# Attention score products cut into column strips of 32 keys, with the diagonal triangles zeroed on GpSimd

## The reference, cut to what matters

```python
b, s, d = x.shape                      # 1, 4096, 256
q = (x @ Wq + bq).reshape(b, s, H, HD).transpose(0, 2, 1, 3)   # H, HD = 16, 16
k = (x @ Wk + bk).reshape(b, s, H, HD).transpose(0, 2, 1, 3)
v = (x @ Wv + bv).reshape(b, s, H, HD).transpose(0, 2, 1, 3)
mask = cols <= rows + WINDOW           # WINDOW = 128
scores = jnp.einsum('bhqd,bhkd->bhqk', q, k) / jnp.sqrt(jnp.float32(HD))
scores = jnp.where(mask[None, None], scores, -jnp.inf)
attn = jax.nn.softmax(scores, axis=-1)
out = jnp.einsum('bhqk,bhkd->bhqd', attn, v)
```

## Time and profile before

| | |
|---|---|
| time, median of 3 runs | 2160.57 us (2159.54 to 2161.64) |
| the profiled execution | 2161.43 us |
| its span, first to last instruction | 2159.7 us |
| first to last exponential of the attention | 222.7 to 1376.6 us |
| PE busy over the span | 1945.6 us (90%) |
| ACT busy over the span | 1349.6 us (62%) |
| DVE, POOL busy over the span | 457.2 us, 206.6 us |

### The profile page before, as it was taken

How to read it: one execution, slowest core, us unless ns; L and a number is a source line. 1 busy time by engine, 2 the same in 40 slices (tenths; PEclk the granted TensorE clock), 3 DMA queues, 4 the chain that set the end, 5 groups by cost and what they waited for, 6 DMA issues and landing times. The chain is left out here.

```text
span 2159.7 us, 33152 instructions
## 1 busy us (share of the span) xinstructions
PE 1945.6 (90%) x11417; PEld 870.4 (40%) x11418; DVE 457.2 (21%) x1360; ACT 1349.6 (62%) x1633; POOL 206.6 (10%) x175
## 2 busy tenths in 40 slices
PE   4863999999999999999999999766299999999995
PEld 3532322223222223222232222255266677667764
DVE  4655000000000000000000000145333333333332
ACT  2432789998989988999988999532133333333331
POOL 1000000000000000000000000146312211221121
PEclk9985999999999999999999999876599999999998
DMA  4336310000300004000000000385422212221223
GB/s 137 124 129 121 70 38 8 9 9 16 76 16 9 8 9 84 9 8 9 8 23 16 8 9 1 116 293 192 146 41 34 34 32 33 33 34 32 34 32 95
DMA packets 83767, 115.15 MB, mean 53 GB/s; under 512 B 9372, under 2 KB 75612, under 8 KB 83036
## 3 DMA queue, kind: packets, MB, share of 16 engines
q1 hardware_dynamic: 66616, 90.97, 14.9%
q0 software_dynamic: 13296, 17.80, 4.8%
q10 hardware_dynamic: 3760, 5.03, 0.8%
HBM read 73.03 MB, written 40.74 MB: 53 GB/s over the span
## 5 line engine op out<-in xcount | busy, mean ns | idle before, releaser
L1034 ACT ACTIVATE at_probs<-at_scores 128x1536 f32<-128x1536 f32 (+2 forms) x756 | 1044.8, 1433 | 113.9 <-PE at_scores L955 55.8
L952 PE MATMUL at_scores<-at_q_rows,kept_k_rows 99*128 99x512 bf16 (+3 forms) x2480 | 613.6, 362 | 10.7 <-DMA at_q_rows<-q_parts 9.4
L969 PE MATMUL at_out<-at_probs,kept_v 128*17 128x512 f32 (+3 forms) x4832 | 593.1, 567 | 0.3 <-ACT at_probs L1034 0.3
L952 PEld LDWEIGHTS at_scores<-at_q_rows,kept_k_rows 99*128 99x128 bf16 x2480 | 193.6, 98 | 621.6 <-ACT at_probs L1034 429.6
L1741 ACT ACTIVATE ex_hT<-ex_ps_hT,kept_b 128x128 f32<-128x128 f32 x568 | 154.5, 383 | 375.1 <-PE ex_ps_hT L1698 375.1
L1706 PE MATMUL ex_ps_y<-kept_w,ex_hT 128*128 x1136 | 258.7, 381 | 2.5 <-ACT ex_hT L1741 2.5
L1687 PE MATMUL ex_ps_h<-kept_w,ex_xT 128*128 x568 | 259.9, 601 | 0.9 <-DVE ex_xT L1756 0.9
L1047 DVE COPY at_out_T<-at_out 128x512 f32<-128x512 f32 x32 | 22.1, 692 | 1047.7 <-PE at_out L969 1047.7
L1706 PEld LDWEIGHTS ex_ps_y<-kept_w,ex_hT 128*128 128x128 f32 x1136 | 211.4, 191 | 28.9 <-issue 2.7
L969 PEld LDWEIGHTS at_out<-at_probs,kept_v 128*17 128x17 f32 x4832 | 82.5, 95 | 218.1 <-issue 207.8
L1666 POOL DMA_INDIRECT sums<-ex_y,ex_answer_to x71 | 110.8, 1560 | 485.8 <-DVE ex_y L1798 485.8
(11 more groups left out here) (209 smaller groups left out, 990.4 us busy)
## 6 DMA issues: line engine op xcount, KB each, us to landing
kept_w<-in_W SPq DMA_DIRECT2D x16, 1024.0 KB, 10.2
ex_x_tile<-queue SPq DMA_DIRECT2D x72, 129.5 KB, 2.0
k_parts<-kparts SPq DMA_DIRECT2D x8, 768.0 KB, 3.7
q_parts<-qparts SPq DMA_DIRECT2D x8, 768.0 KB, 3.7
at_q_rows<-q_parts SPq DMA_DIRECT2D x32, 192.0 KB
kept_k_rows<-k_parts SPq DMA_DIRECT2D x4, 1120.0 KB
x_rows<-in_x SPq DMA_DIRECT2D x4, 1024.0 KB, 14.1
kept_k_rows<-k_parts SPq DMA_DIRECT2D x8, 512.0 KB
```

The costliest lines, as they stand in the source:

```text
L952: ins = nc.tensor.matmul(out, k_rows[:, k_at + h * S + kb * P:k_at + h * S + (kb + 1) * P], q_rows[:, q:q + part], start=True, stop=not ma ...
L969: ins = nc.tensor.matmul(ps_o[h * CT:h * CT + HD + 1, first:C], v[:, kb, g * GH + h, :], probs[:, slot, column:column + width], start=i == ...
L1034: nc.scalar.activation(probs[:, c % RING, 0:width], ps_s[:, c % 2, 0:width], ACT.Exp).then_inc(exped, 1)
```

## The change

The score matmul of a block of 128 keys becomes four matmuls of 32 keys, each with its own weight load; the four write to partitions 0, 32, 64 and 96 of the same columns. The masking matmuls go, and `mask_kq` with them. In their place POOL sets the probabilities above the diagonal to zero in `probs`, in place, after the exponential: one `affine_select` for each step's pieces in a chunk (`edge_runs`), up to four heads of 128 columns. A value product of a diagonal block waits for it (semaphore `masked`). `LAG` goes from 2 to 3, so the products run one chunk later behind the scores, and the transposes too. The rest of the diff are counts of a semaphore in the setup, where one memset and one select go.

```diff
...
-            nc.gpsimd.memset(keep["mask_kq"][:], 0.0).then_inc(pool_step, 1)
             nc.gpsimd.memset(keep["mask_qk"][:], 0.0).then_inc(pool_step, 1)
-            pool.wait_ge(pool_step, 6)
-
-            nc.gpsimd.affine_select(out=keep["mask_kq"][:], in_=keep["mask_kq"][:], compare_op=ALU.is_ge, fill=MASKED,
-                                    base=0, pattern=[[1, P]], channel_multiplier=-1).then_inc(pool_step, 1)
+            pool.wait_ge(pool_step, 5)
+
...
-        LAG = 2
+        LAG = 3
...
+        def edge_runs(tile, n):
+
+            runs = []
+            for i, step in enumerate(tiles[tile]):
+                at = [column for k, h, column in pieces(tile, n) if k == i]
+                if step[0] > tile * CB and at:
+                    runs.append((at[0], step[4], len(at)))
+            return runs
+
+        masks_of = [[len(edge_runs(tile, n)) for n in range(chunks_of[tile])] for tile in range(NC)]
+
+        def masks_upto(g, tile, n):
+
+            return (g * sum(sum(m) for m in masks_of) + sum(sum(m) for m in masks_of[:tile])
+                    + sum(masks_of[tile][:n + 1]))
+
...
                     kb, first, _, _, width = tiles[tile][i]
-                    edge = kb > tile * CB
                     done = 0
                     while done < width:
                         at = column + done
                         part = min(width - done, C - at % C)
-                        out = ps_s[:, c % 2, at:at + part]
-                        masked = edge and done == 0
                         q = q_at + h * C + first + done
-                        ins = nc.tensor.matmul(out, k_rows[:, k_at + h * S + kb * P:k_at + h * S + (kb + 1) * P],
-                                               q_rows[:, q:q + part], start=True, stop=not masked)
-                        if masked:
-                            ins = nc.tensor.matmul(out[:, 0:P], ident_bf[:], mask[:], start=False, stop=True)
+                        k = k_at + h * S + kb * P
+                        for b in range(0, P, CT):
+                            ins = nc.tensor.matmul(ps_s[b:b + CT, c % 2, at:at + part], k_rows[:, k + b:k + b + CT],
+                                                   q_rows[:, q:q + part], start=True, stop=True)
                         done += part
                 ins.then_inc(scored, 1)
...
                 kb, first, width = step[0], step[1], step[4]
+                if kb > tile * CB:
+                    pe.wait_ge(masked, masks_upto(g, tile, place(step, GH - 1)[0]))
...
-                products(c - 1)
-            for upto in (len(order) - 1, len(order)):
+                products(c - LAG + 1)
+            for upto in range(len(order) - LAG + 1, len(order) + 1):
                 pe.wait_ge(exped, upto + 1)
                 products(upto)
             transposes(turn)
+
+        @block.gpsimd
+        def _(pool):
+            for c, (g, tile, n) in enumerate(order):
+                for k, (column, spacing, count) in enumerate(edge_runs(tile, n)):
+                    if k == 0:
+                        pool.wait_ge(exped, c + 2)
+                    part = probs[:, c % RING, column:column + (count - 1) * spacing + P]
+                    if count > 1:
+                        part = probs[:, c % RING, column:column + count * spacing].rearrange(
+                            "p (h q) -> p h q", h=count)[:, :, 0:P]
+                        pattern = [[0, count], [1, P]]
+                    else:
+                        pattern = [[1, P]]
+                    nc.gpsimd.affine_select(out=part, in_=part, compare_op=ALU.is_ge, fill=0.0, base=0,
+                                            pattern=pattern, channel_multiplier=-1).then_inc(masked, 1)
...
```

More of the change, by code:

```diff
@@ L221, in _ @@
                                           w[:, k].rearrange("p (h d) -> p d h", h=H)).then_inc(pool_step, 1)
-            pool.wait_ge(pool_step, 8 + 2 * KD)
+            pool.wait_ge(pool_step, 6 + 2 * KD)
         @block.scalar
@@ L298, in _ @@
             pe.wait_ge(act_step, 3)
-            pe.wait_ge(pool_step, 8 + 2 * KD)
+            pe.wait_ge(pool_step, 6 + 2 * KD)
             pe.wait_ge(w_in, 16 * 6)
@@ L827, in sem @@
             return ctx.enter_context(nc.semaphore(name))
-        ident, ident_bf, mask, v, mixed = (keep[n] for n in ("ident", "ident_bf", "mask_kq", "v", "mixed"))
+        ident, v, mixed = (keep[n] for n in ("ident", "v", "mixed"))
         CT = 32
@@ L858, in attention @@
         pv_done = sem("at_pv_done")
+        masked = sem("at_masked")
         out_read = sem("at_out_read")
@@ L1841, in adaln_attention_experts @@
             kept(inner, "ident_bf", [P, P], BF16)
-            kept(inner, "mask_kq", [P, P], BF16)
             kept(inner, "mask_qk", [P, P], BF16)
```

## The result

The changed kernel takes 2086.59 us, the median of four runs (2084.18 to 2087.97); the kernel before took 2161.11 us beside it (four runs, 2159.54 to 2162.82). The ratio is 0.9654, with a 95% interval of 0.9637 to 0.9671: faster by 74.5 us. The profiled execution is the one of 2084.18 us.

The account below looks back on a forecast made before the run. PE was taken to bound the attention stage, ACT close behind. With joins and masks gone ACT becomes the bound; its wait falls from 108 to 43 us, -65 from the median 2160.57: 2095 us, range 2076 to 2115 (66%).

Parts of the forecast that it names:

- the forecast case: Whole program: the main expectation, 2076 to 2115 us, given 66%.
- The joins: Between scores and value products on PE: 0.10 us lost at each of 2 x 574 goes, 115 us of PE time.
- The strips: Score matmuls on PE: 2480 become passes of four, 5 ns extra each, +12 us; upper end 240 ns a pass, +60 us.
- Rival A: Score strips on PE overlap only in part; halfway, 40 ns extra a pass, PE stays the bound, about 2126 us; 14%.
- Rivals B and C: PE's instruction stream limits: at 90 ns a pair, 2278 us (B, 12%); at 81 ns, unchanged at 2160 us (C, 5%).
- ACT becomes the bound: Attention stage: PE's time falls to 1024 us, under ACT's 1045, so ACT sets the pace.
- the cycle is 5.3 us against 5.57: Inner cycle of four chunks: PE needs 5.3 us, ACT's four exponentials 5.57, so PE waits some 0.27 us.
- What ACT still waits for: Attention stage: ACT's wait for PE falls from 108 us to 43 us, -65 us.
- Tile starts: Turns with the transposes and a tile's first products: ACT waits 0.7 us at each of 31 tiles, 22 us.
- Group starts: First tile of groups 1 to 3: later query loads make PE wait near 4.2 us each, 13 us for three.
- The selects and the lag: Selects on POOL: 0.6 us for 512 columns, hidden with products three chunks behind; upper end up to 20 us.
- The masks: Masking matmuls on PE: 496 go, 0.06 us each, 30 us of PE time.

Follow-up runs that it names:

- run 2: The changed kernel with its scores on the whole array again, selects on POOL and LAG 3 kept: 2141.0 us, 0.9902 of the kernel before.
- run 3: The changed kernel with score strips of 64 columns, value products still on strips of 32: 2154.16 us, 0.9956 of the kernel before.
- Run 4: The changed kernel with every score matmul cut in two along the queries, 19840 in place of 9920: 2115.94 us, 0.9786 of the kernel before.
- run 10: The changed kernel with the exponential over only the first half of each chunk, output not the attention: 2038.56 us, 0.9423 of the kernel before.
- run 5: The changed kernel with LAG 2 in place of 3: 2085.46 us, 0.963 of the kernel before.
- run 1: The kernel before with scores and masking matmuls on strips of 32, no work on POOL, LAG 2: 2111.8 us, 0.9768 of the kernel before.
- run 6: The changed kernel with the next group's key loads spread over tiles 3 to 6: 2082.16 us, 0.9624 of the kernel before.
- run 9: The changed kernel with score matmuls halved along the queries and key loads spread over tiles 3 to 6: 2093.27 us, 0.9676 of the kernel before.
- run 7: The changed kernel with three buffers of query rows in place of two: 2071.76 us, 0.9572 of the kernel before.

## Why the prediction was right, point by point

The time forecast was 2095 us and the measured one 2086.59, faster as predicted and inside the narrower range of the forecast case as well. Its mechanism held; two terms were mis-sized, in opposite directions, and that the time came so close is in part luck: the profiled execution, 2084.2 us, lies 12.2 under 2161.4 - 65, where the larger error by itself is 21.8.

**The joins.** Predicted: 0.1 us each, gone with equal widths, products within 0.02 us of the end of the scores' stream. Shown: 0.86 and 0.65 us in place of 0.99 and 0.75 in the timelines, back in runs 2 and 3. The step held, and run 3 sharpens it: the width must be the same, not merely a strip. The Trainium skill, in TensorEngine Tiling (Array Packing), section Key Properties, says that changing the tiling mode, and not just the tile, drains TensorE. The traces agree in that each such change costs 0.10 to 0.13 us of PE here, while the next group's first weight load doesn't run ahead.

**The strips.** Taken: 5 ns a pass over 216, with 240 ns as the upper end. Shown: twelve matmuls from 642.01 to 642.66 are 0.65 us, no more than three whole ones took, so the extra is nothing that the rows can resolve. Rival A falls; it needed 22 ns.

**PE's instruction stream.** Rivals B and C needed a limit of 81 to 90 ns a pair. Run 4 held 46 ns a pair through the inner part without loss. The 90 ns seen before were PE busy with streaming, as the prediction argued, and not a limit. The Trainium skill, in TensorE: Matmul & The Clock Gate, section Back-to-back issue gap, has about 81 ns for a sustained stream at 128 columns; no run here has such a stream for long, but eight pairs of 128 columns start 60 ns apart, and pairs of 256 and 512 columns on four strips went at 46 ns, so the traces do not bear it out as a limit on issue.

**ACT becomes the bound: right, but its floor was mis-sized.** The step that failed is "the cycle is 5.3 us against 5.57": 5.57 us is the length of four exponentials from the first start to the last end, and the prediction used it as what four take from start to start. The last one's end overlaps the next start when nothing waits. Three starts in 5.57 - 1.45 = 4.12 us are 1.37 us each in that same row, four are 5.49 us, and after it is 5.46. So the stage's floor was not 1045 us: the busy time fell by 21.8 us once the exponentials followed each other without a wait. That is the larger of the two errors, and the row to see it in was there. PE's cycle was forecast too long as well, 5.3 us where run 10 has 5.17, so the margin between the two, 0.27 us, came out right (0.29).

**What ACT still waits for: 43 us predicted, 52.7 found.** Tile starts: 0.20 + 0.56 = 0.76 us against 0.7, right; over the stage, ACT's waits before chunks 4 and 5 add up to 19.1 us against 22. Group starts: 4.74, 4.38 and 4.97 us, 14.1 against 13, about right. Behind them, two chunks on, ACT waited 0.78, 0.81 and 1.48 us, 3.1 against the 4 counted for the low clock. Short last chunks: eight of 0.54 against 0.5. Left out altogether was the wait of 2.40 us on PE while the keys load, which cost ACT 3.23 + 1.47 = 4.7 us. The wait before the very first exponential was left out too: 4.23 us, which was 4.75 before and lies within the 108 us that the 43 were set against. The rest, some 3 us, are small waits.

Put together: the wait fell by 55.2 us and not 65 (9.7 short), and the floor by 21.8 that was not counted. 65.2 - 9.7 + 21.8 = 77.3, the difference of the two profiled executions.

**The selects and the lag.** A select of 512 columns took 635 ns over the stage, against 0.6 us predicted, and was hidden, as predicted. But the reason given for it, three chunks of lag, was not what hid it: run 5 hides it with two. The price of the lag at the group starts was somewhat under-sized: 1.4 us each was predicted, and run 5 gives back 1.6 to 2.5.

**The masks.** The prediction priced 496 masking matmuls at 30 us of PE time. Runs 1 and 2 put the worth of moving them to POOL, with the lag, at 25 and 22 us of the whole, and the 25 hold the waits on issue of run 1.

## What to carry to other kernels

Where short groups of matmuls alternate, look at the distance between their starts beyond what they stream; if the groups use different column widths of the array, cut the wider one to the narrower width: here that cost four times the score instructions and no stream time that the rows can resolve. Before calling an engine's busy time its floor, divide the distance between the starts of a run of instructions, without the last one's length, by one less than their count: recorded durations that overlap make the floor look higher than it is. And where a large load runs beside long unrolled code, look for waits on issue behind it, and try the load in parts over time where its data is not needed for long.

## What the runs showed of the hardware that was not expected

PE stood still behind a large load, for 2.40 us in the kernel after and up to 6.2 us in run 4, waiting for nothing that the profile shows. Runs 6 and 9 show that the load in one piece causes the long waits: spread over four tiles, there is none in run 6, and run 9 keeps 4.7 of run 4's 22.8 us and is 22.7 us faster. Runs 1, 5, 7 and 10, which keep the load in one piece, have them too, 5.4 to 9.6 us in each. That what is late are PE's instructions is argued, not shown: the traffic of the instruction queue grew with the code, from 69 packets and 1.13 MB on the page of before to 124 and 2.03 MB, and so did the waits when run 4 took the code to 67064 instructions. The kernel before, with 33152 instructions, issues the same loads at the same tile, with up to 410 GB/s (269 to 270 us), and has no such wait of PE in its list of waits. Nor has run 3 with 37304. If it is the size of the code that counts, it sets in between that and the 47224 of the kernel after; where was not tried.

A short stop cost more than its length. Behind those 2.40 us the granted clock was 0.50 at 270 and still at 274 us, and ACT paid 4.7 us for them, 2.3 more. At the start of the second group PE stood still for 3.29 us (to 500.31); the granted clock was 0.50 behind it too (503 to 504 us), and ACT paid 4.74 + 0.78 us, 2.2 more. How much of this the clock makes by itself no run parts.
